# The last row group finished in two halves, and the fourth unit of x loaded ahead of the first matrix block

## The chip, the cores and the metric

The kernel runs on 1 core of one Trainium2 chip. The metric is the device time of one execution in microseconds (us). The kernel before takes 378.2 us (median of 3 runs, 377.26 to 378.64).

## The reference, cut to what matters

```python
# N = 5120 rows (2048 users, 3072 items), 64 features, adj is 5120 x 5120, all fp32
h = jnp.maximum(_layernorm(x, axis=-1), 0.0)              # first norm and relu
u = par_u[0] * par_u[1] * (diag_u[:, None] * h_u @ W_u) + h_u
i = par_i[0] * par_i[1] * (diag_i[:, None] * h_i @ W_i) + h_i
e = jnp.concatenate([u, i], axis=0)
o = adj @ (adj.T @ e)                                      # two products with the matrix
mu, var = jnp.mean(o, -1, keepdims=True), jnp.var(o, -1, keepdims=True)
layer = (o - mu) * jax.lax.rsqrt(var + 1e-5) * ln_gamma + ln_beta + h
result = x + layer
```

## The kernel before, in words

**Tiling.** The matrix is handled as 20 panels of 256 columns (`PANELS`, g = 0 to 19) and 5 groups of 1024 rows (`GROUPS`, m = 0 to 4). A block of one panel and one group is 1 MB, and one DMA brings it into `natural` (`load_natural(g, m)`). For each panel, TensorE makes t = panel.T @ e in 40 matmuls of 256 columns (`first`, L641, bank `t_acc`); VectorE centres t (`keep_t`) and ScalarE spreads it. Then the panel is used again for adj @ t. For row groups 0 to 3 (`TURNED`) VectorE turns the block in 32x32 pieces into `strips` (`turn_strips`, L458), and TensorE multiplies from there (`second_strips`, L670, four banks of `h_acc`). For row group 4 (`LOADED`) the turned block is loaded from memory a second time into `cols` (`load_cols`), and TensorE multiplies with it (`second_loaded`, L654, 4 matmuls of 512 columns into bank 4 of `h_acc`). Panels 0 to 3 and the last two are written out; the others run in a loop, two at a time.

**The start.** SyncE issues the loads in one queue, in the order of the code: x unit 0, the small inputs, block (0, 0), x units 3 and 4, block (1, 0), x unit 5, and the eight other blocks of panels 0 and 1, then the first `cols`. ScalarE issues x units 1 and 2. VectorE norms x in six units (`UNITS`, u = 0 to 5): row sums (L410), centring (L416), squares summed (L421), reciprocal (L429), and two steps that make e (L442, L448). Its order is written out by hand: the row sums and the centring of unit 3 stand ahead of the two steps that make e of unit 0. TensorE's first matmul on the matrix waits for e of unit 0.

**The end.** The last panel (19) meets row groups 0 to 3 in another way: its columns come turned from memory (`adj_last`), and `last_columns(m)` (L707) makes the last part of the sum of group m in a bank of its own. VectorE adds it to the rest (`out_sum`, L567), TensorE turns the sum so that rows lie on partitions (`out_turn`, L721), ScalarE squares (L392), VectorE sums the squares (L421), ScalarE takes the root (L314), VectorE takes the reciprocal (L429) and scales (`out_scale`, L583). Gamma is multiplied in by GpSimd for groups 0 and 2 (L293) and by VectorE for groups 1 and 3 (L576, ahead of the scaling). GpSimd adds x, h and beta, which lie ready in `xs` (L296), and SyncE stores the group. `scaled` has two buffers, so from group 2 on VectorE waits for GpSimd's addition of the group two before.

Group 4 comes last: after the last `second_loaded`, ScalarE squares it (L402), matmuls with `ones` sum the squares over the features (`last_var`, L730), VectorE multiplies by gamma where features lie on partitions (L594, `gamma_d`), TensorE turns the product (L721), and VectorE takes the reciprocal, scales (L583), adds (L598), and SyncE stores 256 KB. The lines that wait for the work before it are these:

```python
                if m >= 2:
                    dve.wait_ge(s_o_added, m - 1)      # also m = 4: the third addition on GpSimd
```

## Time and profile before

| what | value |
|---|---|
| median of 3 runs | 378.2 us (377.26 to 378.64) |
| profiled execution, its own time | 377.57 us |
| its span | 375.8 us |
| TensorE busy | 366.2 us (97%) |
| VectorE busy | 252.2 us (67%) |
| ScalarE busy | 73.4 us (20%) |
| GpSimd busy | 22.6 us (6%) |
| moved by DMA | 133.13 MB, mean 354 GB/s |

The span runs from the first to the last event that the profile shows. The execution's own time is 1.8 us more. PE is TensorE, PEld its weight load, DVE is VectorE, ACT is ScalarE, POOL is GpSimd, and SPq is the DMA queue of SyncE. A row of the timeline reads: start, duration, engine, line, operation, output and inputs, shapes, and how often. A bracket at its end is idle time of the engine just ahead of it, with what ended it. An fp32 matmul instruction leaves two records, a transpose one. Each timeline used here is that of one engine; records of one kind that follow each other are merged into one row.

### The profile page before, as it was taken

The numbers are of one execution on the slowest core, as the hardware profiler recorded it, in microseconds if no ns is written. First come the engines' busy times: TensorE is split into PE (matmuls) and PEld (weight loads), VectorE is DVE, ScalarE is ACT, GpSimd is POOL, SyncE is SP. The second block draws the span as 40 slices with busy tenths as digits, with TensorE's granted clock in tenths as the row PEclk, the third lists the DMA queues.
The fourth block names the chain that finished last, engine by engine and source line by source line (L and its number), as shares of the span: only waits on it lengthen the run. The fifth ranks groups of instructions, "written<-read, shape, count | busy, mean of one in ns | idle before, by whom it ended". The sixth has DMA issues, their size and how long they took to land.

```text
span 375.8 us, 9724 instructions
## 1 busy us (share of the span) xinstructions
PE 366.2 (97%) x4328; PEld 192.0 (51%) x4328; DVE 252.2 (67%) x242; ACT 73.4 (20%) x212; POOL 22.6 (6%) x29
## 2 busy tenths in 40 slices
PE   7899999999999999999999999999999999999994
PEld 4565454545643664465456436634654464456332
DVE  4999995759528933992496279339933982622476
ACT  5763022200220022003102200220022023002321
POOL 2024060000000000000000000000000000000035
PEclk9999999999999999999999999999999999999999
DMA  8999999999999999699959986996999599949003
GB/s 310 420 421 415 419 423 419 419 421 419 420 418 419 374 425 425 232 399 426 425 194 413 424 368 261 425 423 240 385 426 424 207 421 427 380 133 413 17 13 128
DMA packets 19746, 133.13 MB, mean 354 GB/s; under 512 B 2192, under 2 KB 2704, under 8 KB 3856
## 3 DMA queue, kind: packets, MB, share of 16 engines
q1 hardware_dynamic: 19440, 132.48, 86.2%
q10 hardware_dynamic: 288, 0.39, 0.3%
q8 instruction: 13, 0.21, 0.2%
q14 instruction: 5, 0.04, 0.0%
HBM read 131.55 MB, written 1.31 MB: 354 GB/s over the span
## 4 chain that ended last, share of the span: by engine, by line
PE 87%; DVE 6%; issue 1%; ACT 0%; DVEq 0%
PE t_acc L641 41%; PE h_acc L670 35%; PE h_acc L654 9%; DVE strips L458 2%; PE t_acc L707 1%; DVE var L421 1%; DVE scaled L583 1%; DVE e L442 1%; DVE natural L567 0%; PE h_acc L721 0%; DVE e L448 0%; DVE scaled L576 0%; DVE centred L471 0%; DVE rstd L429 0%; DVE xs L598 0%
## 5 line engine op out<-in xcount | busy, mean ns | idle before, releaser
L458 DVE STREAM_TRANSPOSE strips<-natural 128x2048 f32<-128x2048 f32 x76 | 168.2, 2275 | 49.3 <-PE h_acc L670 49.3
L641 PE MATMUL t_acc<-natural,e 128*64 128x256 f32 x1600 | 175.7, 380 | 0.7 <-DVE e L448 0.3
L641 PEld LDWEIGHTS t_acc<-natural,e 128*64 128x64 f32 x1600 | 114.3, 137 | 63.3 <-issue 6.3
L670 PE MATMUL h_acc<-strips,centred 32*64 32x512 f32 x2432 | 133.3, 589 | 0.1
L670 PEld LDWEIGHTS h_acc<-strips,centred 32*64 32x64 f32 x2432 | 53.4, 132 | 78.4 <-issue 77.9
L338 ACT COPY t_high<-t_acc 64x256 f32<-64x256 f32 x20 | 7.4, 368 | 211.7 <-PE t_acc L641 211.7
L466 DVE TENSOR_TENSOR t_sum<-t_acc,t_high 64x256 f32<-64x256 f32 x20 | 8.2, 410 | 56.3 <-ACT t_high L338 56.0
L654 PE MATMUL h_acc<-cols,centred 128*64 128x512 f32 x160 | 38.3, 599 | 0.0
L345 ACT COPY centred<-centred 32x384 f32<-32x384 f32 (+2 forms) x60 | 24.2, 403 | 67.3 <-DVE centred L479 66.8
L346 ACT COPY centred<-centred 32x128 f32<-32x128 f32 (+2 forms) x60 | 23.9, 398 | 0.0
L293 POOL TENSOR_TENSOR scaled<-scaled,smalls 128x512 f32<-128x512 f32 x2 | 2.5, 1270 | 310.6 <-DVE scaled L583 310.6
L654 PEld LDWEIGHTS h_acc<-cols,centred 128*64 128x64 f32 x160 | 10.5, 136 | 20.3 <-issue 19.1
L471 DVE STREAM_TRANSPOSE centred<-t_sum 32x256 f32<-32x256 f32 x40 | 17.3, 432 | 1.0
L479 DVE SCALAR_TENSOR_TENSOR centred<-t_total,centred 32x512 f32<-32x512 f32 x20 | 13.6, 679 | 0.7
L477 DVE TENSOR_REDUCE t_total<-centred 32x8 f32<-32x512 f32 x20 | 13.5, 674 | 0.7
L330 ACT ACTIVATE strips<-centred,rstd 128x64 f32<-128x64 f32 x40 | 10.0, 335 | 1.1 <-DVE rstd L429 1.1
L276 POOL TENSOR_TENSOR xs<-xs,strips 128x512 f32<-128x512 f32 x5 | 6.2, 1270 | 20.7 <-DVE e L448 20.7
L282 POOL TENSOR_TENSOR xs<-xs,smalls 128x512 f32<-128x512 f32 x5 | 6.2, 1282 | 14.5 <-issue 14.5
L421 DVE TENSOR_REDUCE var<-squares 128x8 f32<-128x512 f32 (+1 forms) x10 | 6.3, 627 | 0.8 <-ACT squares L392 0.5
L410 DVE TENSOR_REDUCE total<-xs 128x8 f32<-128x512 f32 (+1 forms) x6 | 3.6, 593 | 4.7 <-DMA xs<-x 4.6
L618 PE MATMUL h_acc<-ident,centred 128*128 128x128 f32 x20 | 3.8, 306 | 2.0 <-DVE centred L416 2.0
L629 PE MATMUL h_acc<-smalls,across 128*128 128x128 f32 x40 | 5.4, 283 | 0.3 <-ACT across L323 0.3
(53 smaller groups left out, 77.2 us busy)
## 6 DMA issues: line engine op xcount, KB each, us to landing
natural<-adj_rows SPq DMA_DIRECT2D x100, 1024.0 KB, 11.7
cols<-adj_cols SPq DMA_DIRECT2D x20, 1024.0 KB, 13.4
natural<-adj_last SPq DMA_DIRECT2D x4, 1024.0 KB, 7.2
out<-xs SPq DMA_DIRECT2D x5, 256.0 KB, 2.0
xs<-x SPq DMA_DIRECT2D x3, 256.0 KB, 7.4
xs<-x ACTq DMA_DIRECT2D x1, 256.0 KB, 3.5
smalls<-small SPq DMA_DIRECT2D x1, 150.0 KB, 3.2
xs<-x ACTq DMA_DIRECT2D x1, 128.0 KB, 2.9
```

Source lines behind the costliest of these rows:

```text
L330: last = nc.scalar.activation(h_in[:, k], centred_of(u)[:, n], ACT.Relu, scale=rstd[:, u % 2, n:n + 1])
L345: nc.scalar.copy(part[:, :, 0:QUADRANTS - q], t[0:Q, a, :, q:QUADRANTS])
L346: last = nc.scalar.copy(part[:, :, QUADRANTS - q:QUADRANTS], t[0:Q, a, :, 0:q])
L421: nc.vector.tensor_reduce(var[:, n % 2, 0:tiles], squares[:, n % 2, 0:tiles], AX.X, ALU.add).then_inc(s_var, 1)
L458: nc.vector.transpose(strips[:, a, :, m].rearrange("p c t i -> p t c i"), natural[:, a, m].rearrange("p t (c j) -> p t c j", j=Q)).then_in ...
L466: nc.vector.tensor_tensor(t_sum[:], t_acc[0:D, a, 0:WIDE], t_high[:], ALU.add).then_inc(s_t_sum, 1)
L471: last = nc.vector.transpose(t[0:Q, a, :, :, Q * d:Q * (d + 1)], t_sum[Q * d:Q * (d + 1), :].rearrange("p (b u j) -> p b u j", b=BLOCKS, j=Q))
L477: nc.vector.tensor_reduce(t_total[:], rows, AX.X, ALU.add).then_inc(s_t_total, 1)
L479: nc.vector.scalar_tensor_tensor(rows, t_total[:].unsqueeze(2).to_broadcast([Q, STRIPS, D]), -1.0 / D, rows, ALU.mult, ALU.add).then_inc(s ...
L641: last = nc.tensor.matmul(t_acc[D * s:D * (s + 1), a, 0:WIDE], e[:, GT * m + 2 * k + s, :], natural[:, a, m, HALF * s + k], start=(m == 0 ...
L654: last = nc.tensor.matmul(h_acc[D * s:D * (s + 1), LOADED], t[:, a, b, 0, :], cols[:, a, s, b], start=(isinstance(g, int) and g == 0 and b ...
L670: last = nc.tensor.matmul(h_acc[D * s:D * (s + 1), q], t[part, a, b, u, :], rows, start=(isinstance(g, int) and g == 0 and b == 0 and u == 0),
```

## The change

It has two parts. At the start, the load of x unit 3 is issued ahead of matrix block (0, 0). At the end:

- The 512 loaded columns of row group 4 are two parts of 256. Part 0 of the last two panels goes to a new bank, `late`; what had gathered for it before is copied out early (`kept`), and VectorE adds the two (`part_sum`). Part 1 stays in bank 4.
- Each part is squared, multiplied by gamma (on ScalarE, for both parts), turned, and finished by itself. The finish is a reciprocal and four `scalar_tensor_tensor` instructions of 64 elements (times reciprocal, plus `xs`), in the place of one scaling and one addition of 512. Each part is stored by itself (128 KB).
- The turning of group m on TensorE stands between the halves of `last_columns(m + 1)`, no longer behind the whole of it.
- Gamma of group 1 moves from VectorE to GpSimd.

```diff
             load_x(0)
             sp.dma_start(smalls[:, 0:GAMMA], small[:, 0:GAMMA]).then_inc(s_small, 16)
+            load_x(3)
             load_natural(0, 0)
-            load_x(3)
             load_x(4)
...
-            for m in range(GROUPS):
-                if m < LOADED:
-                    sp.wait_ge(s_o_added, m + 1)
-                else:
-                    sp.wait_ge(s_o_done, 1)
+            for m in range(TURNED):
+                sp.wait_ge(s_o_added, m + 1)
                 sp.dma_start(out[:, rows_of(m), :], xs[:, rows_of(m), :]).then_inc(s_out, 16)
+            for part in range(2):
+                sp.wait_ge(s_o_done, part + 1)
+                sp.dma_start(out[:, last_rows(part), :], xs[:, last_rows(part), :]).then_inc(s_out, 16)
...
-                if m % 2 == 0:
-                    nc.gpsimd.tensor_tensor(scaled[:, 0], scaled[:, 0], gamma_s.unsqueeze(1).to_broadcast([P, GT, D]),
+                if m < LOADED - 1:
+                    nc.gpsimd.tensor_tensor(scaled[:, m % 2], scaled[:, m % 2],
+                                            gamma_s.unsqueeze(1).to_broadcast([P, GT, D]),
                                             ALU.mult).then_inc(s_o_pool_gamma, 1)
...
+            def last_square(part, h):
+                nc.scalar.activation(across[:, 1, columns_of(part)], h, ACT.Square).then_inc(s_last_square, 1)
+
+            def last_gamma(part, h):
+                nc.scalar.activation(across[:, 0, columns_of(part)], h, ACT.Copy,
+                                     scale=gamma_d).then_inc(s_last_copy, 1)
...
             for m in range(TURNED):
                 square_out(m)
+                if m == TURNED - 1:
+                    act.wait_ge(s_part_sum, 1)
+                    last_square(0, h_part)
+                    act.wait_ge(s_norm, 16)
+                    last_gamma(0, h_part)
+                std(LATER + m)
+            act.wait_ge(s_part_done, 2)
+            last_square(1, h_acc[:, LOADED, columns_of(1)])
+            last_gamma(1, h_acc[:, LOADED, columns_of(1)])
+            for part in range(2):
+                act.wait_ge(s_last_var, part + 1)
+                nc.scalar.activation(var[:, 0, halves(part)], last_vars(part), ACT.Sqrt, bias=eps[:],
+                                     scale=1.0 / D).then_inc(s_std, 1)
...
+            def part_sum():
+
+                dve.wait_ge(s_part_done, 1)
+                dve.wait_ge(s_kept, 1)
+                nc.vector.tensor_tensor(h_part, late[:, columns_of(0)], kept, ALU.add).then_inc(s_part_sum, 1)
+
+            def last_rows_out(part):
+                n = LATER + LOADED + part
+                dve.wait_ge(s_std, n + 1)
+                nc.vector.reciprocal(rstd[:, 0, halves(part)], var[:, 0, halves(part)]).then_inc(s_rstd, 1)
+                dve.wait_ge(s_rstd, n + 1)
+                dve.wait_ge(s_o_turned, LOADED + part + 1)
+                for k in range(HALF):
+                    at = HALF * part + k
+                    row = xs[:, GT * LOADED + at]
+                    last = nc.vector.scalar_tensor_tensor(row, last_bank(part)[:, D * k:D * (k + 1)], rstd[:, 0, at:at + 1],
+                                                          row, ALU.mult, ALU.add)
+                last.then_inc(s_o_done, 1)
...
             out_scale(2)
+            part_sum()
             out_scale(3)
-            dve.wait_ge(s_last_square, 1)
-            nc.vector.tensor_scalar(across[:, 0], h_acc[:, LOADED], gamma_d, None, ALU.mult).then_inc(s_last_copy, 1)
-            out_scale(LOADED)
-            dve.wait_ge(s_o_scaled, GROUPS)
+            dve.wait_ge(s_o_added, LOADED - 1)
             dve.wait_ge(s_res, GROUPS)
-            nc.vector.tensor_tensor(xs[:, rows_of(LOADED), :], scaled[:, LOADED % 2], xs[:, rows_of(LOADED), :],
-                                    ALU.add).then_inc(s_o_done, 1)
+            for part in range(2):
+                last_rows_out(part)
...
-            last_columns(0)
-            last_columns(1)
-            out_turn(0)
-            last_columns(2)
-            out_turn(1)
-            last_columns(3)
-            out_turn(2)
-            second_loaded(LAST - 1, 0, LAST // 2)
-            out_turn(3)
-            second_loaded(LAST, 1, LAST // 2)
-            last_var()
-            out_turn(LOADED)
+            last_columns(0, range(BLOCKS))
+            for m in range(1, TURNED):
+                last_columns(m, range(1))
+                out_turn(m - 1)
+                last_columns(m, range(1, BLOCKS))
+            loaded_part(0, 0)
+            out_turn(TURNED - 1)
+            loaded_part(0, 1)
+            loaded_part(1, 0)
+            loaded_part(1, 1, range(1))
+            last_turn(0)
+            loaded_part(1, 1, range(1, BLOCKS))
+            for part in range(2):
+                last_var(part)
+            last_turn(1)
```

On TensorE, at the start of the end stage, the kernel before runs the columns of groups 0 and 1 (L707) whole, then the transposes of group 0 (L721):

```order
L707 MATMUL t_acc<-natural,centred 64x512 [waits s_t,s_t_sum,s_natural00]
L707 MATMUL t_acc<-natural,centred 64x512 x3
L707 MATMUL t_acc<-natural,centred 64x512 [waits s_natural01]
L707 MATMUL t_acc<-natural,centred 64x512 x3
L721 MATMUL h_acc<-ident,natural 128x128 [waits s_o_sum]
L721 MATMUL h_acc<-ident,natural 128x128 x3
```

In the changed kernel the same place of TensorE reads as follows (L776 is `last_columns`, L795 `out_turn`):

```order
L776 MATMUL t_acc<-natural,centred 64x512 [waits s_t,s_t_sum,s_natural00]
L776 MATMUL t_acc<-natural,centred 64x512 x3
L776 MATMUL t_acc<-natural,centred 64x512 [waits s_natural01]
L776 MATMUL t_acc<-natural,centred 64x512
L795 MATMUL h_acc<-ident,natural 128x128 [waits s_o_sum]
L795 MATMUL h_acc<-ident,natural 128x128 x3
L776 MATMUL t_acc<-natural,centred 64x512 x2
```

Four transposes that wait for the sum of group 0 now stand ahead of the last two matmuls of group 1. The same pattern comes again for groups 1 and 2.

On VectorE, the kernel before ends like this, from the squares of group 3 on:

```order
L421 TENSOR_REDUCE var<-squares 128x8 [waits s_squares]
L576 TENSOR_TENSOR scaled<-t_acc,smalls 128x512 [waits s_o_added]
L429 RECIPROCAL rstd<-var 128x8 [waits s_std]
L583 TENSOR_TENSOR scaled<-scaled,rstd 128x512 [waits s_o_gamma,s_rstd]
L594 TENSOR_SCALAR across<-h_acc,smalls 128x512 [waits s_last_square]
L429 RECIPROCAL rstd<-var 128x8 [waits s_std,s_o_added]
L583 TENSOR_TENSOR scaled<-h_acc,rstd 128x512 [waits s_o_turned,s_rstd]
L598 TENSOR_TENSOR xs<-scaled,xs 128x512 [waits s_res,s_o_scaled]
```

The changed kernel, from `part_sum` (L627) on, ends like this on the same engine (L460, L468, L616 and L621 are L421, L429, L576 and L583 of before):

```order
L627 TENSOR_TENSOR natural<-late,natural 128x256 [waits s_kept,s_part_done]
L460 TENSOR_REDUCE var<-squares 128x8 [waits s_squares]
L616 TENSOR_TENSOR scaled<-t_acc,smalls 128x512 [waits s_o_added]
L468 RECIPROCAL rstd<-var 128x8 [waits s_std]
L621 TENSOR_TENSOR scaled<-scaled,rstd 128x512 [waits s_o_gamma,s_rstd]
L632 RECIPROCAL rstd<-var 128x4 [waits s_std,s_res,s_o_added]
L638 SCALAR_TENSOR_TENSOR xs<-h_acc,rstd,xs 128x64 [waits s_o_turned,s_rstd]
L638 SCALAR_TENSOR_TENSOR xs<-h_acc,rstd,xs 128x64 x3
L632 RECIPROCAL rstd<-var 128x4 [waits s_std]
L638 SCALAR_TENSOR_TENSOR xs<-h_acc,rstd,xs 128x64 [waits s_o_turned,s_rstd]
L638 SCALAR_TENSOR_TENSOR xs<-h_acc,rstd,xs 128x64 x3
```

The gamma of group 4 (L594) is gone from VectorE. The wait for GpSimd's third addition (`s_o_added`) still stands ahead of the first reciprocal of group 4. Three instructions behind that wait have become ten.

## Rows read from the trace of the kernel before

**Rows 1.** The page: the span, and what the DMA engines moved in 40 equal slices.

```profile
span 375.8 us, 9724 instructions
GB/s 310 420 421 415 419 423 419 419 421 419 420 418 419 374 425 425 232 399 426 425 194 413 424 368 261 425 423 240 385 426 424 207 421 427 380 133 413 17 13 128
```

**Rows 2.** Timeline of PE, the first 36 us.

```profile
11.87 1.08 PE L641 MATMUL t_acc<-natural,e 128*64 128x256 f32 x8 [0.35 <-DVE e L448]
...
33.10 1.95 PE L641 MATMUL t_acc<-natural,e 128*64 128x256 f32 x16 [0.32 <-DMA natural<-adj_rows]
35.16 7.13 PE L670 MATMUL h_acc<-strips,centred 32*64 32x512 f32 x128
```

**Rows 3.** Timeline of DVE, the first 12 us, and 18 to 34 us.

```profile
9.40 0.69 DVE L410 TENSOR_REDUCE total<-xs 128x8 f32<-128x512 f32 x1 [1.14 <-DMA xs<-x]
...
18.82 0.16 DVE L436 TENSOR_TENSOR rstd_diag<-rstd,smalls 128x8 f32<-128x8 f32 x1
18.89 0.20 DVE L429 RECIPROCAL rstd<-var 128x8 f32<-128x8 f32 x1
...
32.76 11.06 DVE L458 STREAM_TRANSPOSE strips<-natural 128x2048 f32<-128x2048 f32 x5
```

**Rows 4.** Timeline of PE, the end stage.

```profile
359.07 0.66 PE L721 MATMUL h_acc<-ident,natural 128*128 128x128 f32 x4
359.66 1.94 PE L707 MATMUL h_acc<-natural,centred 128*64 128x512 f32 x8
```

**Rows 5.** Timeline of DVE, the end stage.

```profile
357.53 0.69 DVE L567 TENSOR_TENSOR natural<-t_acc,natural 128x512 f32<-128x512 f32 x1 [0.57 <-PE t_acc L707]
359.19 0.69 DVE L567 TENSOR_TENSOR natural<-t_acc,natural 128x512 f32<-128x512 f32 x1 [0.97 <-PE t_acc L707]
360.39 0.69 DVE L421 TENSOR_REDUCE var<-squares 128x8 f32<-128x512 f32 x1 [0.52 <-ACT squares L392]
...
364.31 1.39 DVE L583 TENSOR_TENSOR scaled<-scaled,rstd 128x512 f32<-128x512 f32 x1
...
370.20 0.74 DVE L594 TENSOR_SCALAR across<-h_acc,smalls 128x512 f32<-128x512 f32 x1
371.44 0.20 DVE L429 RECIPROCAL rstd<-var 128x8 f32<-128x8 f32 x1 [0.50 <-POOL xs L296]
371.76 0.69 DVE L583 TENSOR_TENSOR scaled<-h_acc,rstd 128x512 f32<-128x512 f32 x1
372.49 0.70 DVE L598 TENSOR_TENSOR xs<-scaled,xs 128x512 f32<-128x512 f32 x1
```

**Rows 6.** Timeline of POOL, the end stage.

```profile
362.52 1.27 POOL L293 TENSOR_TENSOR scaled<-scaled,smalls 128x512 f32<-128x512 f32 x1 [309.33 <-DVE scaled L583]
363.88 1.27 POOL L296 TENSOR_TENSOR xs<-scaled,xs 128x512 f32<-128x512 f32 x1
...
368.33 1.27 POOL L293 TENSOR_TENSOR scaled<-scaled,smalls 128x512 f32<-128x512 f32 x1 [1.28 <-DVE scaled L583]
369.68 2.95 POOL L296 TENSOR_TENSOR xs<-scaled,xs 128x512 f32<-128x512 f32 x2
```

**Rows 7.** Windows near the end; the last two columns are DMA share and GB/s.

```profile
373.00:373.50 0.50, 0.00 (x0) 0.00 (x0) 0.19 (x1) 0.00 (x0) 0.00 (x0) 1.00 0.05 16
373.50:374.00 0.50, 0.00 (x0) 0.00 (x0) 0.00 (x0) 0.00 (x0) 0.00 (x0) 1.00 0.99 369
...
374.50:375.00 0.50, 0.00 (x0) 0.00 (x0) 0.00 (x0) 0.00 (x0) 0.00 (x0) 0.50 0.76 283
```

**Rows 8.** Timeline of SyncE's queue, the last 12 us.

```profile
365.18 8.37 SPq L257 DMA_DIRECT2D out<-xs  x5
```

**Rows 9.** Groups by shape, whole span: busy, mean ns of one.

```profile
L330 ACT ACTIVATE strips<-centred,rstd 128x64 f32<-128x64 f32 x40 | 10.0, 335 | 1.1 <-DVE rstd L429 1.1
...
L448 DVE TENSOR_TENSOR e<-e,strips 128x512 f32<-128x512 f32 x4 | 2.8, 689 | 0.1
...
L448 DVE TENSOR_TENSOR e<-e,strips 128x256 f32<-128x256 f32 x2 | 0.8, 424 | 0.1
```

125 lines of the change are left out of this document (82 added, 43 removed).

## The prediction

> **What bounds the kernel now.** I read the page first: TensorE is 97% busy, and the DMA engines move some 420 GB/s over the first 120 us [rows 1]. I then looked only at the two places that the change touches, the first 35 us and the last 20. Everything between them stays as it is, and TensorE runs there without a gap that the waits show.
>
> At the start, VectorE idles 1.14 us at 9.40 for x unit 3, and behind that stands e of unit 0, for which TensorE starts its first matmuls on the matrix at 11.87 [rows 2, 3]. So unit 3 does hold back the first matmul. But a second wait comes later: at 33.10 TensorE idles 0.32 us for a matrix block, the last of panel 1, and only two row groups' worth (1.95 us) later does `second_strips` begin, at 35.16 [rows 2]. That block is the last of ten of 1.05 MB. With x (1.31 MB) and the small inputs (0.15 MB) 11.95 MB stand ahead of its landing. The four first slices of 9.4 us carry 310, 420, 421 and 415 GB/s [rows 1], so 12.8 MB have moved by 33.1 us. The queue has been full all the time: the block comes when the bytes ahead of it have come.
>
> At the end, the last step that waits is at 371.44: the reciprocal of group 4 idled 0.50 us for GpSimd's third addition [rows 5]. On GpSimd, gamma of group 0 starts at 362.52, gamma of group 2 at 368.33, and two additions fill 369.68 to 372.63 [rows 6]; the first of these ends at 371.41 and releases VectorE. Then come 0.20 us of reciprocal, a scaling at 371.76 and an addition that ends at 373.19. The last of the stores is issued at 373.22 (the queue's row ends at 373.55, less 0.33 of one issue; five issues share the row) [rows 8]. The stores of groups 3 and 4, 512 KB, move their bytes from 373.5 to 374.88: the window before has a share of 0.05, the window from 373.50 has 0.99, the one from 374.50 has 0.76 [rows 7]. The span ends at 375.8, 0.92 us after the last byte.
>
> **The start, step by step.** With unit 3 ahead of block (0, 0), its 0.26 MB no longer wait behind 1.05 MB. VectorE has its 1.14 us back, unless unit 3 still comes late (0.93 MB at 0.42 MB per us are 2.2 us of queue; it is needed at 8.3). So e of unit 0 and the first matmul come about 1.1 us earlier. All that TensorE does up to 33.10 can shift by as much. The last block of panel 1 can't: the same bytes stand ahead of it. TensorE then idles 0.32 + 1.1 = 1.4 us there, and the gain is gone. What is left: in the kernel before, VectorE's strips of block (0, 3), the first of five in the row at 32.76, end at about 35.05, together with TensorE [rows 3]. If VectorE is 1.1 us ahead, `second_strips` follows the matmuls directly, at some 35.0 instead of 35.16. I take −0.2 us. The bounds are 0 (the strips are late anyway) and −1.1 (the block lands earlier too, so that all of the shift is kept).
>
> **The end on TensorE.** The number of columns is the same. Halving the matmuls costs nothing by the rows: 16 records of 256 columns take 1.95 us [rows 2], 8 of 512 take 1.94 [rows 4]. What moves is `out_turn`. The transposes of group 0 take 0.59 us of TensorE (359.07 to 359.66) [rows 4]. They now stand ahead of the last two matmuls of group 1, and wait for VectorE's sum of group 0, ready at 358.22 [rows 5], while TensorE would be there at 358.1: a wait of 0.1 to 0.2. So group 1's columns are done not at 359.14 but 0.8 later, at 359.95. VectorE runs in order: the sum of group 1 (359.19 before, 360.0 now) stands ahead of group 0's sum of squares. The squares come earlier (the transposes do), but the sum of squares can start only 0.6 after the sum of group 1 does, at 360.6 instead of 360.39 [rows 5]. Group 0 is scaled 0.2 us later, though its transposes were moved up.
>
> **The end on GpSimd.** It has one instruction more, gamma of group 1. Up to the third addition it runs six of 1.27 us with gaps of up to 0.09 [rows 6]: 362.73 + 6 × 1.27 + 0.4 = 370.75. The kernel before had idle time in this stretch (1.28 us ahead of 368.33), which the new instruction fills. Then there is the port that the two engines share: VectorE's scaling of group 1, with both tensors in SBUF, took 1.39 us instead of 0.69 at 364.31, while GpSimd's addition ran to 365.15 [rows 5, 6], and GpSimd's addition at 369.68 took 1.73 because such a scaling ran. By my walk through the order, the scaling of group 3 is ready at 369.3, waits until gamma of group 2 ends at 369.4, and runs then; the third addition is held by 0.55 and ends at 371.3. Before, it ended at 371.41: −0.1. The fourth addition ends at 372.6 (372.63 before), so the store of group 3 is issued as before.
>
> **The end on VectorE.** Gamma of groups 1 and 4 goes (0.68 and 0.74 us), `part_sum` comes (0.42, by the 128x256 row [rows 9]). All that lies under the wait for GpSimd and moves nothing; `kept` lies in VectorE's idle time ahead of 355.66. ScalarE's two gammas and the last roots are ready by 371.2 in my walk, 0.1 us early: a thin cover, which costs its own excess if it fails. Behind the wait stand a reciprocal and four instructions, twice. The trace has no `scalar_tensor_tensor` of 128x64 with a pointer as scalar. By length: 0.689 at 512 and 0.424 at 256 [rows 9] give 0.0010 us per element, so 0.22 at 64. The pointer: L594, which has one, took 0.744 [rows 5], 0.06 more than its neighbours. I take 0.28 each. With no wait between, the next starts before the last ends: at 18.82 one of 0.16 is followed after 0.07 [rows 3]. So four take 3 × 0.19 + 0.28 = 0.85. The bounds are 3 × 0.13 + 0.22 = 0.61 (no pointer cost) and 4 × 0.335 = 1.34 (ScalarE's 128x64 with a pointer [rows 9], no overlap).
>
> The chain is then: 371.35 reciprocal; 371.67 first of the four (0.32 behind, as 371.44 to 371.76); end 372.52; the second reciprocal at 372.45; its four from 372.77 to 373.62. Before, VectorE ended at 373.19. That is 0.43 later (bounds 0.0 and 1.4).
>
> The Trainium skill (VectorE: DVE Perf Modes, The DRAIN you can't avoid) says that the next Vector instruction does not start until the pipe has emptied, and its rules for kernel authors say to minimize the number of instructions. By that rule, four would take 4 × 0.28 = 1.12 us, and the end would come 0.5 us later than in my sum; the row at 18.82 speaks against it here.
>
> **The stores.** Part 1's store is issued at 373.65. Store of group 3 and part 0 (384 KB) have the DMA engines from 373.5 to 374.54, at the 1.38 us that 512 KB took [rows 7]. Group 3's bytes moved 0.85 us after its issue (372.65 to 373.5), so part 1 can move from 374.5, just when they come free, to 374.88. This is the end of before. A VectorE up to 0.4 us late costs nothing, and one that is earlier gains nothing, since the fourth addition on GpSimd still sets when the last 512 KB begin. End: 0.0, bounds −0.1 and +1.0 (VectorE at its upper bound, 1.4 − 0.4).
>
> **Sum.** −0.2 (start) and 0.0 (end): 377.57 becomes 377.4 for the profiled execution. The median of the runs shown is 0.63 above that execution: 378.0.
>
> **The rivals.**
> 1. *The start's gain is kept.* For it: unit 3 is the wait at 9.40. It needs the last block of panel 1 to land 1.1 us earlier, with the same bytes ahead of it. 0.9 MB beyond these had moved by then, so landing isn't strictly in order, and a little may shift. 376.9, and 376.0 if the end gave 0.9 too. Chance 0.20.
> 2. *The small instructions cost more,* at the upper bound without overlap, or the last roots are late: +0.7 to +1.0, 379.0. Chance 0.12.
> 3. *Slower: the port.* The eight small instructions read and write `xs` in SBUF while the fourth addition runs (371.3 to 372.6). If they count as such a pair, they start at 372.6, 0.95 later, and with the upper price of each the end moves to 372.6 + 1.34 + 0.5 + 1.34 = 375.8, 2.2 us past the point from which it counts: 380.2. At my price of each it is 374.8, so 379.1. It decides from a start behind 372.0. For it: the 1.39 at 364.31. Against it: L594, with a pointer in SBUF, ran in its usual time at 370.20 beside GpSimd. The Trainium skill (SBUF — State Buffer, Terms) has the pair of ports locked for the whole of an instruction, the other engine blocked, which the 1.39 bears out. Chance 0.09.
> 4. *The interleaved transposes add up:* each of three waits 0.2 for VectorE, and scaling of all groups comes 0.6 later: 378.6. Chance 0.07.
>
> The forecast itself has 0.52. Its own range is 377.2 to 378.9, with the spread of the runs. Faster by over 0.5% would be below 376.3, slower above 380.1; 0.5% is about what a measurement of this kernel can tell from no change. Faster takes a third of rival 1 and a little from the rest: 0.09. Slower takes half of rival 3 and little more: 0.06. The range of 8 in 10 takes in most of rivals 1 and 2: 376.7 to 379.3.
>
> **What the profile of the changed kernel would show.** First matmul on the matrix at 10.8 with no idle of VectorE ahead of unit 3's row sums; then an idle of some 1.4 us for a block near 33.1, and `second_strips` at 35.0. If that row stands at 34.0, rival 1 is right. At the end: the first scaling 0.2 later, GpSimd without idle from 362.7 to its last addition but for the held one, the reciprocal of part 0 released by GpSimd at 371.1 to 371.3 (after the start's shift), small instructions of 0.22 to 0.34. A reciprocal released by ScalarE, or small instructions of over 0.5, would show the forecast wrong.

## The result and the profile after

The changed kernel takes 378.67 us (median of 17 executions, 377.9 to 379.25); the kernel before, taken beside it, 377.59 us (17 executions). The ratio is 1.002 with an interval of 1.0011 to 1.0029. The change costs 1.1 us (0.3%) by the medians and 0.8 us (0.4 to 1.1) by the ratio. The forecast was no change with a gain of 0.2 us within it. The profiled execution took 378.85 us, its span 377.0 us; what lies outside the span is 1.85 us in this one.

The page of the changed kernel, the two lines that answer to [rows 1]:

```profile
span 377.0 us, 9769 instructions
GB/s 263 427 417 417 420 423 418 421 421 417 421 420 418 365 428 424 244 395 429 421 213 411 429 356 249 428 423 242 359 428 422 227 388 427 407 146 408 11 14 127
```

The first slice of 9.4 us carries 263 GB/s where it was 310. The next twelve slices differ from those of before by at most 7 GB/s, in both directions. So the DMA engines fall behind by 0.44 MB in the first 9.4 us, and don't make it up in the slices behind it.

The changed kernel, timeline of TensorE, the first 36 us (columns as in [rows 2]; L696 is `first`, L727 `second_strips`):

```profile
10.57 1.08 PE L696 MATMUL t_acc<-natural,e 128*64 128x256 f32 x8 [0.26 <-DVE e L487]
...
29.30 1.95 PE L696 MATMUL t_acc<-natural,e 128*64 128x256 f32 x16 [0.40 <-DMA natural<-adj_rows]
31.79 1.95 PE L696 MATMUL t_acc<-natural,e 128*64 128x256 f32 x16 [0.54 <-DMA natural<-adj_rows]
34.35 1.95 PE L696 MATMUL t_acc<-natural,e 128*64 128x256 f32 x16 [0.61 <-DMA natural<-adj_rows]
36.22 7.12 PE L727 MATMUL h_acc<-strips,centred 32*64 32x512 f32 x128
```

The first matmul on the matrix comes at 10.57, 1.30 us earlier than in [rows 2]. Then TensorE waits for three blocks one after the other, where it waited once, and `second_strips` begins at 36.22, not at 35.16: 1.06 us later. The next view says what happened to the blocks.

The changed kernel, windows at the start (columns: PE busy, PEld, DVE, ACT, POOL, granted clock, DMA share, GB/s):

```profile
2.00:10.00 8.00, 6.74 (x43) 4.37 (x40) 6.21 (x15) 5.47 (x17) 0.70 (x2) 1.00 0.97 338
5.00:6.00 1.00, 0.91 (x6) 0.43 (x4) 1.00 (x3) 0.49 (x2) 0.07 (x1) 1.00 1.01 217
10.00:28.00 18.00, 16.90 (x141) 11.08 (x141) 16.40 (x31) 12.31 (x45) 2.27 (x2) 1.00 1.02 422
```

From 2 to 10 us the DMA engines moved 338 GB/s; the kernel before moved 394 there, and 401 between 5 and 6 us, where the changed one has 217. The share of busy time is about 1 in both (0.97 and 1.00 from 2 to 10 us). By the share the engines were taken, but they brought fewer bytes. From 10 us on the rate is 422, as before (421).

On VectorE the row sums of unit 3 no longer wait (they start at 8.12), but those of unit 5 do:

```profile
13.10 0.69 DVE L449 TENSOR_REDUCE total<-xs 128x8 f32<-128x512 f32 x1 [1.26 <-DMA xs<-x]
```

So VectorE's lead is gone again: its strips that began at 32.76 in [rows 3] begin at 32.63.

The changed kernel, timeline of TensorE at the end stage (L776 is `last_columns`, L795 `out_turn`):

```profile
356.54 2.80 PE L776 MATMUL t_acc<-natural,centred 128*64 128x512 f32 x12
359.33 0.65 PE L795 MATMUL h_acc<-ident,natural 128*128 128x128 f32 x4
359.92 1.08 PE L776 MATMUL t_acc<-natural,centred 128*64 128x512 f32 x4
```

The end stage starts at 356.54, where the kernel before had 355.49: the 1.05 us of the start, carried through the whole kernel without a change. For the end I therefore compare times counted from this row. The end stage lasts 20.46 us up to the end of the span, and 20.31 before.

The changed kernel, timeline of VectorE, the last 5 us ([rows 5] of before):

```profile
369.50 0.68 DVE L616 TENSOR_TENSOR scaled<-t_acc,smalls 128x512 f32<-128x512 f32 x1
370.10 0.19 DVE L468 RECIPROCAL rstd<-var 128x8 f32<-128x8 f32 x1
370.32 1.78 DVE L621 TENSOR_TENSOR scaled<-scaled,rstd 128x512 f32<-128x512 f32 x1
372.03 0.16 DVE L632 RECIPROCAL rstd<-var 128x4 f32<-128x4 f32 x1
372.23 0.86 DVE L638 SCALAR_TENSOR_TENSOR xs<-h_acc,rstd,xs 128x64 f32<-128x64 f32 x4
373.01 0.17 DVE L632 RECIPROCAL rstd<-var 128x4 f32<-128x4 f32 x1
373.21 0.86 DVE L638 SCALAR_TENSOR_TENSOR xs<-h_acc,rstd,xs 128x64 f32<-128x64 f32 x4
```

The changed kernel, timeline of GpSimd, the same stretch ([rows 6] of before):

```profile
368.93 1.28 POOL L316 TENSOR_TENSOR scaled<-scaled,smalls 128x512 f32<-128x512 f32 x1
370.29 1.26 POOL L320 TENSOR_TENSOR xs<-scaled,xs 128x512 f32<-128x512 f32 x1
372.19 1.26 POOL L320 TENSOR_TENSOR xs<-scaled,xs 128x512 f32<-128x512 f32 x1 [0.63 <-DVE scaled L621]
```

GpSimd's third addition starts at 370.29, VectorE's scaling of group 3 at 370.32. Both have their tensors in SBUF. The addition runs in its usual 1.26, the scaling takes 1.78 where one alone takes 0.69. The last stretch of VectorE is then released by its own scaling, no longer by GpSimd: the reciprocal at 372.03 has no idle ahead of it. VectorE ends at 374.07, or 17.53 after the start of the stage; before it was 373.19, or 17.70.

The changed kernel, timeline of SyncE's queue, the last stores (L277 stores groups 0 to 3, L280 the two parts):

```profile
366.42 7.39 SPq L277 DMA_DIRECT2D out<-xs  x4
373.85 1.40 SPq L280 DMA_DIRECT2D out<-xs  x2
```

The changed kernel, windows at the end (columns as above):

```profile
374.50:375.00 0.50, 0.00 (x0) 0.00 (x0) 0.00 (x0) 0.00 (x0) 0.00 (x0) 0.50 0.94 356
375.00:375.50 0.50, 0.00 (x0) 0.00 (x0) 0.00 (x0) 0.00 (x0) 0.00 (x0) 0.50 0.51 172
375.50:376.00 0.50, 0.00 (x0) 0.00 (x0) 0.00 (x0) 0.00 (x0) 0.00 (x0) 0.50 0.79 262
376.00:377.00 1.00, 0.00 (x0) 0.00 (x0) 0.00 (x0) 0.00 (x0) 0.00 (x0) 0.50 0.17 55
```

The issues by line say how long each of them took (minimum, median and maximum in ns, then the start of the first and of the last):

```profile
L280 SPq DMA_DIRECT2D out<-xs x2: 439/676/912, 373.8 to 374.8; - x2
L277 SPq DMA_DIRECT2D out<-xs x4: 332/338/348, 366.4 to 373.5; - x4
```

A store of 256 KB takes 0.34 us to issue. Those of the two halves take 0.91 and 0.44. The row of 1.40 runs from 373.85 to 375.25, and the last of the two starts at 374.8, so the long one is part 0's. The share falls to 0.51 between the stores of part 0 and part 1. So VectorE was 0.17 earlier, counted from the stage's start, and the span 0.15 later.

A third piece doesn't show in any row. The time of an execution less its span is 1.75 to 2.00 us in all 134 executions of the kernel before whose span is known, with a mean of 1.86 to 1.92 by batch. (One of them took 994.47 us and is in none of the medians and ratios.) In the changed kernel it is over 2.2 in 6 of 17 (up to 2.9), with a mean of 2.17. The median of the spans is 376.2 for the changed kernel and 375.6 to 375.7, by batch, for the kernel before (its 17 executions above have no spans on record). So the median execution has 0.6 more of span and about 0.3 more outside it. Together that is 0.9, between the 0.8 of the ratio and the 1.1 of the medians. The profiled execution has 1.2 more of span, 1.05 from the start and 0.15 from the end: the start cost more in it than in the middle one.

### The profile page after: what moved, and what is told of

Same layout as the page of the kernel before. It is cut to its first block, busy times and chain, and to the rows that moved or that the text cites. A ratio compares the mean times of both kernels' runs of the same rounds, so it can differ in the third digit from the quotient of the medians.

```text
span 377.0 us, 9769 instructions
## 1 busy us (share of the span) xinstructions
PE 366.9 (97%) x4344; PEld 192.3 (51%) x4344; DVE 252.2 (67%) x249; ACT 74.3 (20%) x216; POOL 23.4 (6%) x30
## 4 chain that ended last, share of the span: by engine, by line
PE 87%; DMA 7%; DVE 2%; SPq 2%; issue 1%; ACT 0%; DVEq 0%
PE t_acc L696 42%; PE h_acc L727 35%; PE h_acc L710 9%; DMA natural<-adj_rows 7%; SPq L230 1%; PE t_acc L776 1%; PE h_acc L776 1%; DVE var L460 0%; DVE scaled L621 0%; SPq L227 0%; DVE xs L638 0%; DVE natural L608 0%; PE h_acc L795 0%; ACT var L338 0%; DVE scaled L616 0%
## 5 line engine op out<-in xcount | busy, mean ns | idle before, releaser
L696 PE MATMUL t_acc<-natural,e 128*64 128x256 f32 x1600 | 176.2, 380 | 1.8 <-DMA natural<-adj_rows 1.6
L696 PEld LDWEIGHTS t_acc<-natural,e 128*64 128x64 f32 x1600 | 114.1, 137 | 65.1 <-issue 6.3
L727 PE MATMUL h_acc<-strips,centred 32*64 32x512 f32 x2432 | 133.3, 589 | 0.0
L727 PEld LDWEIGHTS h_acc<-strips,centred 32*64 32x64 f32 x2432 | 52.9, 132 | 78.7 <-issue 77.9
L710 PE MATMUL h_acc<-cols,centred 128*64 128x512 f32 x144 | 34.4, 598 | 0.0
L316 POOL TENSOR_TENSOR scaled<-scaled,smalls 128x512 f32<-128x512 f32 x3 | 3.8, 1275 | 310.7 <-DVE scaled L621 310.7
L710 PEld LDWEIGHTS h_acc<-cols,centred 128*64 128x64 f32 x144 | 9.5, 136 | 18.9 <-issue 17.6
L460 DVE TENSOR_REDUCE var<-squares 128x8 f32<-128x512 f32 (+1 forms) x10 | 6.3, 626 | 0.3 <-ACT squares L334 0.2
L684 PEld LDWEIGHTS h_acc<-smalls,across 128*128 128x128 f32 x40 | 4.8, 191 | 2.0 <-ACT across L347 1.3
```

Source lines behind the costliest of these rows:

```text
L684: last = nc.tensor.matmul(unit_bank(u)[:, P * b:P * (b + 1)], across[:, u % 2, P * b:P * (b + 1)], wdiag[:, int(lo >= N_USERS // P)], star ...
L696: last = nc.tensor.matmul(t_acc[D * s:D * (s + 1), a, 0:WIDE], e[:, GT * m + 2 * k + s, :], natural[:, a, m, HALF * s + k], start=(m == 0 ...
L710: last = nc.tensor.matmul(h_acc[D * s:D * (s + 1), LOADED], t[:, a, b, 0, :], cols[:, a, s, b], start=(isinstance(g, int) and g == 0 and b ...
L727: last = nc.tensor.matmul(h_acc[D * s:D * (s + 1), q], t[part, a, b, u, :], rows, start=(isinstance(g, int) and g == 0 and b == 0 and u == 0),
```

## The experiments

Each median stands beside that of the kernel before, taken on the same chip, with the ratio's interval. "Span" is the median of the spans of all executions, 9 to 12 of each kernel. "Outside" is the mean of an execution's time less its span. Three chips were used: one for e1 to e4, one for e5 to e8 and e13 to e16, one for e9 to e12.

### Which half of the change costs: e1 and e2

`e1_after_x3_back` is the changed kernel with x unit 3 behind the block again:

```diff
-            load_x(3)
             load_natural(0, 0)
+            load_x(3)
             load_x(4)
```

> The changed kernel with x unit 3 back behind matrix block (0, 0); the end stage stays changed. Theory 'start' (with unit 3 ahead, the DMA engines move some 0.4 MB less in the first 9 us though they are busy, so the last block of panel 1 lands 1.2 us later and TensorE waits for it): TensorE's last matmuls of panel 1 (34.35 us in the changed kernel) are back at about 33.1, the first slice of the page is back at some 310 GB/s, and the time is 0.9 to 1.2 us under the changed kernel, 0 to 0.3 over the kernel before. Theory 'end' (the timed difference comes from the end stage, and the late block is chance of one execution): the time stays at 1.0 over the kernel before. Theory 'both': half and half, 0.5 over.

`e2_before_x3_ahead` is the kernel before with that one line moved forward:

```diff
+            load_x(3)
             load_natural(0, 0)
-            load_x(3)
             load_x(4)
```

> The kernel before with x unit 3 ahead of matrix block (0, 0) and nothing else. Theory 'start': 0.9 to 1.2 us slower than the kernel before, with TensorE waiting for matrix blocks 0.4 to 0.6 us three times between 29 and 35 us. Theory 'end': no change within 0.2 us.

Measured: e1 377.91 against 377.57, ratio 1.0011 (1.0000 to 1.0023), span 375.8. e2 378.11 against 377.57, ratio 1.002 (1.001 to 1.0029), span 376.2. By the spans the line alone costs what the whole change costs (376.2 in both); by the medians it costs 0.54 us, half of it. I had expected 0.9 to 1.2 us and three waits for blocks; there are two. Windows of e2 (columns as above):

```profile
2.00:10.00 8.00, 6.32 (x42) 4.16 (x39) 6.08 (x15) 5.46 (x16) 0.69 (x2) 1.00 0.93 345
5.00:6.00 1.00, 0.50 (x4) 0.20 (x2) 1.00 (x3) 0.73 (x3) 0.20 (x1) 1.00 0.71 246
```

The loss of bytes is there too, and in e1 it is not: 376 GB/s from 2 to 10 us and 434 from 5 to 6. Timeline of TensorE in e2, the last block of panel 1:

```profile
33.71 1.95 PE L641 MATMUL t_acc<-natural,e 128*64 128x256 f32 x16 [0.61 <-DMA natural<-adj_rows]
35.59 7.12 PE L670 MATMUL h_acc<-strips,centred 32*64 32x512 f32 x128
```

`second_strips` begins 0.43 later than before here, and at 35.10 in e1. The end stage of e1 lasts 20.08 us in its profile, 0.23 less than before; by the median of its spans, 375.8 against 375.6, nothing of that remains. What e1 still loses, 0.3 us, lies outside the span: 2.26 in the mean, five of eleven executions over 2.2; e2 has 1.90 and none. A difference of this size in the medians says little by itself: `e6_names_only`, further down, does the same work as the kernel before and has 0.34 us more.

### Why the blocks come later: e4, e5, e9 and e10

Theory: x unit 3 directly ahead of block (0, 0) makes the queue carry fewer bytes. Rival: any x unit that is moved forward delays the blocks by its own bytes. Four orders of the kernel before tell these apart. In e4 all three units stand ahead:

```diff
+            load_x(3)
+            load_x(4)
+            load_x(5)
             load_natural(0, 0)
-            load_x(3)
-            load_x(4)
             load_natural(1, 0)
-            load_x(5)
```

> The kernel before with x units 3, 4 and 5 all ahead of the first matrix block. Theory 'pieces': loads of x (pieces of 2 KB and less) that follow each other without a matrix block (pieces of 8 KB) between them move fewer bytes per time. Then this order loses more than unit 3 alone: the last block of panel 1 lands 2 us or more later, time +1.5 to +3. Rival 'one collision' (the loss belongs to the place where unit 3 and unit 2 of the other queue meet): the loss stays at about 1.0. Rival 'bytes' (only the bytes ahead count): no change.

In e5 unit 3 is taken out of SyncE's queue and issued by ScalarE:

```diff
             load_natural(0, 0)
-            load_x(3)
...
-            for u in (1, 2):
+            for u in (1, 2, 3):
                 act.dma_start
```

> The kernel before with x unit 3 issued by ScalarE, behind its units 1 and 2, so that matrix block (0, 0) stays first in SyncE's queue. Theory 'alternation' (the loss comes from SyncE's order unit 3, block, unit 4, block, unit 5: moved all ahead, the units cost nothing): no loss here, the first slice stays at 300 to 310 GB/s, span as before (375.6 median) or down to 0.2 less, since VectorE gets unit 3 early. Theory 'unit 3 early' (whatever brings unit 3 in before block (0, 0) costs): the span rises by 0.6 as with unit 3 ahead.

In e9 units 3 and 4 stand ahead:

```diff
+            load_x(3)
+            load_x(4)
             load_natural(0, 0)
-            load_x(3)
-            load_x(4)
             load_natural(1, 0)
```

> The kernel before with x units 3 and 4 ahead of block (0, 0) in SyncE's queue, unit 5 still behind block (1, 0). With unit 3 alone ahead the DMA engines move 340 to 345 GB/s from 2 to 10 us and the span rises by 0.6; with units 3, 4 and 5 ahead 380, and nothing is lost. If the loss comes from a block that follows one unit of x and is followed by another (unit, block, unit, block, unit), this order has it once and not twice: 355 to 375 GB/s, span +0.2 to +0.4. If it comes from unit 5 between the blocks, the loss is whole: +0.6. If it belongs to unit 3 directly ahead of block (0, 0), none: 375 to 390 GB/s and a span within 0.2.

In e10 only unit 3 does, and unit 4 goes behind block (1, 0):

```diff
+            load_x(3)
             load_natural(0, 0)
-            load_x(3)
-            load_x(4)
             load_natural(1, 0)
+            load_x(4)
             load_x(5)
```

> The kernel before with x unit 3 ahead of block (0, 0), and units 4 and 5 behind block (1, 0). If the loss belongs to unit 3 directly ahead of block (0, 0), it is whole here: 335 to 355 GB/s from 2 to 10 us, span +0.5 to +0.7. If it comes from unit 4 between the two blocks, it is gone: 375 to 390 GB/s. Units 4 and 5 come later for VectorE, which may wait 1 to 2 us for unit 4; the wait for the last block of panel 1 hides that, unless e of the later groups comes late for TensorE.

The table holds the result of each and its windows; "start" is the start of `second_strips` in the profile. e3, which stands under "The stores", has the start of the changed kernel. The ten others are e1, e6 to e8 and e11 to e16, whose edits leave the order of the loads as it was before.

| order | median, before | ratio (interval) | span | GB/s 2 to 10 us | GB/s 5 to 6 us | start |
|---|---|---|---|---|---|---|
| before | | | 375.6 | 394 | 401 | 35.16 |
| after | 378.67, 377.59 | 1.002 (1.0011 to 1.0029) | 376.2 | 338 | 217 | 36.22 |
| the ten others with the order of before | | | | 373 to 397 | 369 to 451 | 34.81 to 35.61 |
| e3, unit 3, changed end | 378.13, 377.57 | 1.0019 (1.0005 to 1.0034) | 376.2 | 346 | 279 | 36.55 |
| e2, unit 3 | 378.11, 377.57 | 1.002 (1.001 to 1.0029) | 376.2 | 345 | 246 | 35.59 |
| e10, unit 3, then two blocks | 379.43, 377.63 | 1.0042 (1.0023 to 1.006) | 377.55 | 355 | 270 | 35.69 |
| e9, units 3 and 4 | 377.78, 377.63 | 0.9999 (0.9985 to 1.0014) | 375.8 | 381 | 412 | 34.90 |
| e4, units 3, 4, 5 | 377.63, 377.57 | 1.0002 (0.9993 to 1.0012) | 375.75 | 380 | 381 | 35.17 |
| e5, unit 3 by ScalarE | 377.66, 377.49 | 1.0003 (0.9994 to 1.0013) | 375.7 | 388 | 430 | 35.22 |

The two windows of e9, and under them those of e10:

```profile
2.00:10.00 8.00, 6.74 (x42) 4.21 (x39) 6.04 (x15) 5.31 (x16) 0.70 (x2) 1.00 1.00 381
5.00:6.00 1.00, 0.92 (x6) 0.44 (x4) 1.00 (x3) 0.33 (x2) 0.28 (x1) 1.00 1.17 412
```

```profile
2.00:10.00 8.00, 7.37 (x33) 4.68 (x30) 6.12 (x15) 4.53 (x13) 0.70 (x2) 1.00 0.96 355
5.00:6.00 1.00, 1.00 (x6) 0.52 (x4) 1.00 (x3) 0.33 (x2) 0.24 (x1) 1.00 0.84 270
```

The rival falls: e4 puts three units ahead, 0.79 MB, and loses nothing. The dip belongs to the orders in which exactly one unit stands between the small inputs and block (0, 0): four profiles with 217 to 279 GB/s between 5 and 6 us, against 369 and more in the fourteen others. With a second unit behind it, or with the first in another queue, it is not there. In e2, e3 and e10 part of the loss is idle time (shares of 0.71, 0.89 and 0.84 between 5 and 6 us), in the changed kernel it isn't (1.01). The share isn't a strict fraction of time: it reads 1.17 in a window of e9.

The column "start" needs more care, since it is one execution of each kernel. With the order of before it varies by 0.8 us (34.81 to 35.61), and 35.59 (e2) and 35.69 (e10) lie at the edge of that; 36.22 and 36.55 lie outside it. What the order costs in time is therefore better read from the spans of e2, +0.6. e10 loses most in its median, more than its start in the profile explains. There unit 4 comes late too, and VectorE waits for it. Timeline of VectorE in e10:

```profile
12.25 0.69 DVE L410 TENSOR_REDUCE total<-xs 128x8 f32<-128x512 f32 x1 [1.16 <-DMA xs<-x]
```

Its spans range from 376.3 to 378.5, and the profiled execution is the shortest of them, so the rest of that loss isn't seen in a row.

None of these orders gains. e9 has the first matmul early and nearly all of the bytes, and yet the last block of panel 1 comes when it did before. Timeline of TensorE in e9:

```profile
10.74 1.08 PE L641 MATMUL t_acc<-natural,e 128*64 128x256 f32 x8 [0.26 <-DVE e L448]
...
33.02 1.95 PE L641 MATMUL t_acc<-natural,e 128*64 128x256 f32 x16 [0.58 <-DMA natural<-adj_rows]
```

It is the same in e4 (first matmul at 10.65, `second_strips` at 35.17). In e5, unit 3 is early too (row sums at 8.44 without a wait), but the first matmul comes at 11.71, so there is little to lose. Timeline of TensorE in e5:

```profile
33.34 1.95 PE L640 MATMUL t_acc<-natural,e 128*64 128x256 f32 x16 [0.59 <-DMA natural<-adj_rows]
35.22 7.12 PE L669 MATMUL h_acc<-strips,centred 32*64 32x512 f32 x128
```

That is the part of the prediction that held: what is gained ahead of the first matmul is lost at this block. The kernels with the order of before say the same without any edit there. VectorE's wait for unit 3 was 1.14 us in the profile of [rows 3], but it is 0 in e7 and e14 and 1.49 in e16. Their first matmuls come at 10.71, 10.80 and 12.31, and `second_strips` at 35.02, 34.87 and 35.61: of the 1.5 to 1.6 us that lie between them at the first matmul, 0.6 to 0.7 are left. So the wait that the change was to remove isn't there in every execution.

### The parts of the end: e7, e8, e15, e14 and e13

`e7_order_and_gamma` is the kernel before with the transposes between the halves of `last_columns` and gamma of group 1 on GpSimd; group 4 is finished as before.

```diff
-                if m % 2 == 0:
-                    nc.gpsimd.tensor_tensor(scaled[:, 0], scaled[:, 0], gamma_s.unsqueeze(1).to_broadcast([P, GT, D]),
+                if m < LOADED - 1:
+                    nc.gpsimd.tensor_tensor(scaled[:, m % 2], scaled[:, m % 2], gamma_s.unsqueeze(1).to_broadcast([P, GT, D]),
...
-            last_columns(1)
-            out_turn(0)
-            last_columns(2)
-            out_turn(1)
-            last_columns(3)
-            out_turn(2)
+            for m in range(1, TURNED):
+                last_columns(m, range(1))
+                out_turn(m - 1)
+                last_columns(m, range(1, BLOCKS))
```

> The kernel before with two parts of the changed end: the transposes of group m between the halves of the columns of group m + 1, and gamma of group 1 on GpSimd; group 4 is finished whole, as before. By my walk the first scaling comes 0.2 later, GpSimd's third addition runs at once and the scaling of group 3 waits for it, so that VectorE's gamma of group 4 and its end come later: end stage 20.4 to 20.9 us from the first columns of group 0 to the end of the span, against 20.31; time 0.1 to 0.6 over before. If executions with over 2.2 us outside the span appear here, they belong to these two parts; if not, to the halves of group 4.

`e8_halves_only` is e1 without these two: group 4 in halves, two stores, the transposes behind the whole of `last_columns`, gamma of group 1 on VectorE.

```diff
-                if m < LOADED - 1:
+                if m % 2 == 0:
                     nc.gpsimd.tensor_tensor(
...
-                last_columns(m, range(1))
-                out_turn(m - 1)
-                last_columns(m, range(1, BLOCKS))
+                last_columns(m, range(BLOCKS))
+                out_turn(m - 1)
```

> The changed kernel with x unit 3 back, the transposes of a group behind the whole columns of the next, and gamma of group 1 on VectorE, as in the kernel before: what is left of the change is group 4 in two halves. The first scaling is back 0.2 earlier, the scaling of group 1 waits for GpSimd again (1.39 us). If it is the halves that gain at the end (0.2 us of span in the kernel with unit 3 back), the end stage is 20.0 to 20.2. Executions with over 2.2 us outside the span: 3 or more of 11 if they belong to the halves, none if to the other parts.

Measured: e7 378.47 against 377.49, ratio 1.0023 (1.0013 to 1.0033), span 376.5. e8 378.5, ratio 1.0028 (1.0018 to 1.0037), span 376.7. Each half of the end alone costs 0.9 to 1.1 us of span, and both together (e1) 0.2 or less. I had expected 0.1 to 0.6 us for e7 and an end stage of 20.0 to 20.2 us for e8, which has 21.57 in its profile: both were missed. Timeline of VectorE in e7:

```profile
369.14 1.76 DVE L583 TENSOR_TENSOR scaled<-scaled,rstd 128x512 f32<-128x512 f32 x1
370.83 0.74 DVE L594 TENSOR_SCALAR across<-h_acc,smalls 128x512 f32<-128x512 f32 x1
...
372.71 0.69 DVE L583 TENSOR_TENSOR scaled<-h_acc,rstd 128x512 f32<-128x512 f32 x1 [1.03 <-PE h_acc L723]
```

With one more instruction GpSimd starts its third addition at 369.10, 0.04 ahead of VectorE's scaling of group 3, and VectorE is held for 1.1 us. Gamma of group 4 stands behind that scaling on VectorE, the last transposes wait for it on TensorE, and VectorE waits for those: 1.03 us. In the changed kernel that gamma is on ScalarE, so the hold delays nothing but VectorE's own end. In e8 the scaling of group 3 starts 14.60 us after the stage's start (13.79 in e1, 14.10 before), since VectorE has both gamma of group 1 and `part_sum` ahead of it. GpSimd's addition is 0.23 us ahead of it (369.50), and it is held all the same. VectorE then ends 0.63 us later against the stage's start than before, and from there to the end of the span it is 3.24 us where it was 2.61; that second part is taken up under "The stores". Timeline of VectorE in e8:

```profile
369.73 1.58 DVE L621 TENSOR_TENSOR scaled<-scaled,rstd 128x512 f32<-128x512 f32 x1
...
372.60 0.86 DVE L638 SCALAR_TENSOR_TENSOR xs<-h_acc,rstd,xs 128x64 f32<-128x64 f32 x4
```

`e15_small_finish` is the kernel before, with eight instructions of 64 elements in the place of the last scaling and addition, and one store:

```diff
-            out_scale(LOADED)
...
-            nc.vector.tensor_tensor(xs[:, rows_of(LOADED), :], scaled[:, LOADED % 2], xs[:, rows_of(LOADED), :],
-                                    ALU.add).then_inc(s_o_done, 1)
...
+            for k in range(GT):
+                row = xs[:, GT * LOADED + k]
+                last = nc.vector.scalar_tensor_tensor(row, out_bank(LOADED)[:, D * k:D * (k + 1)], rstd[:, 0, k:k + 1],
+                                                      row, ALU.mult, ALU.add)
+            last.then_inc(s_o_done, 1)
```

> The kernel before with group 4 finished by one reciprocal and eight instructions of 128x64 in the place of a scaling and an addition, stored once. Eight take 7 x 0.19 + 0.28 = 1.6 us by the row of four in 0.86, against 1.43 before: VectorE ends 0.2 later, span +0.1 to +0.3. Theory 'VectorE' (it is these instructions, or their number): 3 or more of 11 executions with over 2.2 us outside; by the run with wide halves, which had 6 of 12, I expect none.

`e14_gamma_on_scalar` is the kernel before with gamma of group 4 on ScalarE:

```diff
+            nc.scalar.activation(across[:, 0], h_acc[:, LOADED], ACT.Copy, scale=gamma_d).then_inc(s_last_copy, 1)
...
-            nc.vector.tensor_scalar(across[:, 0], h_acc[:, LOADED], gamma_d, None, ALU.mult).then_inc(s_last_copy, 1)
```

> The kernel before with gamma of group 4 on ScalarE (an activation of 128x512 behind the square) in the place of VectorE's instruction. The transposes of group 4 can start at 370.4 instead of 371.0, but the reciprocal still waits for GpSimd's third addition at 371.4, so the span stays within 0.15 of before. Theory 'ScalarE' (one activation more with a pointer as scale): 3 or more of 11 executions with over 2.2 us outside. Rival: none.

`e13_columns_in_halves` is the kernel before with the loaded columns of the last two panels in matmuls of 256:

```diff
...
+                for part in range(2):
+                    at = slice(WIDE * part, WIDE * (part + 1))
+                    for b in range(BLOCKS):
+                        for s in range(2):
+                            last = nc.tensor.matmul(h_acc[D * s:D * (s + 1), LOADED, at], t[:, a, b, 0, :],
+                                                    cols[:, a, s, b, at], start=False,
...
```

> The kernel before, with the loaded columns of the last two panels multiplied as 256 and 256 (16 matmul instructions for 8) into the same bank, and nothing else. By the rows halving costs TensorE nothing: span within 0.1 of before. Theory 'TensorE' (the longer program of TensorE makes the close longer at times): 3 or more of 11 executions with over 2.2 us outside the span. Rival 'elsewhere': none.

Measured against 377.5: e15 377.48, ratio 1.0002 (0.9993 to 1.0011), span 375.7; e14 377.49, ratio 1.0002 (0.9993 to 1.0012), span 375.6. Neither moves the time. Timeline of VectorE in e15, and under it of e14, the same place:

```profile
371.25 0.20 DVE L429 RECIPROCAL rstd<-var 128x8 f32<-128x8 f32 x1 [0.50 <-POOL xs L296]
371.58 1.63 DVE L601 SCALAR_TENSOR_TENSOR xs<-h_acc,rstd,xs 128x64 f32<-128x64 f32 x8
```

```profile
371.15 0.20 DVE L431 RECIPROCAL rstd<-var 128x8 f32<-128x8 f32 x1 [1.16 <-POOL xs L296]
```

Eight small instructions take 1.63 us, and the two of 512 elements with the wait between took 1.43 (371.76 to 373.19, [rows 5]). In e14 the 0.74 us that VectorE no longer needs become idle time: 1.16 where [rows 5] have 0.50. e13 gives 377.76, ratio 1.0023 (1.0007 to 1.0039). The matmuls themselves cost nothing, as this row of TensorE shows:

```profile
364.70 1.95 PE L668 MATMUL h_acc<-cols,centred 128*64 128x256 f32 x16
```

The median is 0.27 higher, the mean more, since 5 of 12 spans are 376.8 to 378.4. I have no row that says why. For this step the run is inconclusive.

### The stores: e3, e11 and e12

`e3_one_store` is the changed kernel with one store of 256 KB behind both parts:

```diff
-            for part in range(2):
-                sp.wait_ge(s_o_done, part + 1)
-                sp.dma_start(out[:, last_rows(part), :], xs[:, last_rows(part), :]).then_inc(s_out, 16)
+            sp.wait_ge(s_o_done, 2)
+            sp.dma_start(out[:, rows_of(LOADED), :], xs[:, rows_of(LOADED), :]).then_inc(s_out, 16)
...
```

> The changed kernel with row group 4 stored once (256 KB, when both parts are done) in the place of two stores of 128 KB. In the changed kernel the issue of part 0's store took 0.91 us and that of part 1 0.44, where the 256 KB stores take 0.33, so that part 1's bytes move only from 375.25. Theory 'small stores cost': the store is issued at 374.1, takes 0.33, lands 2.0 to 2.4 later, and the time is 0.3 to 0.6 us under the changed kernel. Rival 'issue is held by the store before it, whatever the size': the one store's issue takes 0.7 or more and the time is within 0.2 us of the changed kernel.

`e12_x3_back_one_store` is e1 with the same edit, so that the start is that of before:

> The changed kernel with x unit 3 back and group 4 stored once. Theory 'small stores': the span is 0.1 to 0.3 under that with unit 3 back and two stores, so 375.5 to 375.7, level with the kernel before; the time is over before only by the executions with more outside the span, 0 to 0.4. Rival 'no price': the span stays at 375.8.

`e11_halves_wide` is e1 with each part finished by a scaling and an addition of 256 elements:

```diff
-                for k in range(HALF):
-                    at = HALF * part + k
-                    row = xs[:, GT * LOADED + at]
-                    last = nc.vector.scalar_tensor_tensor(row, last_bank(part)[:, D * k:D * (k + 1)], rstd[:, 0, at:at + 1],
-                                                          row, ALU.mult, ALU.add)
...
+                nc.vector.tensor_tensor(scaled[:, 0, halves(part)], last_bank(part).rearrange("p (k d) -> p k d", d=D),
+                                        by_tile(rstd[:, 0, halves(part)]), ALU.mult).then_inc(s_o_scaled, 1)
+                dve.wait_ge(s_o_scaled, LOADED + part + 1)
+                nc.vector.tensor_tensor(rows, scaled[:, 0, halves(part)], rows, ALU.add).then_inc(s_o_done, 1)
```

> The changed kernel with x unit 3 back, and each half of group 4 finished by one scaling and one addition of 128x256 (and a wait between them) in the place of four instructions of 128x64. By the rows, 0.42 + 0.04 + 0.42 = 0.88 against 0.86: time and span as with unit 3 back (span 375.8 median, within 0.3). Executions with over 2.2 us outside the span: if they belong to the eight small instructions, which have no waits between them, none here; if to the halves otherwise, 3 to 5 of 11.

Measured: e3 378.13 against 377.57, ratio 1.0019 (1.0005 to 1.0034), span 376.2, the median of the changed kernel (in the mean 0.17 below it, which is within the scatter). e12 377.55 against 377.63, ratio 0.9994 (0.998 to 1.0008), span 375.3: 0.5 below e1, and 0.4 below the kernel before. But `e16_more_at_the_close`, in the next part, has one store too, and its span is 376.2. So the runs don't show that one store is better than two.

The rows say where these kernels part. In the changed kernel, e1, e3, e12 and e16 VectorE ends 17.51 to 17.54 us after the start of the end stage, all alike. From there to the end of the span it is 2.93 and 2.56 us with two stores (the changed kernel, e1) and 2.52, 3.08 and 3.53 with one (e3, e12, e16). The short ones are those in which each issue of the last stores was short: 0.45 and 0.43 in e1, 0.33 in e3, against 0.91 (part 0), 0.94 and 0.79. The end of e8 (3.24, with 0.86 for part 0) fits that, the end of e11 (2.80, with 1.42 for part 0) less so. Why an issue takes long isn't known; there is one profile of each kernel, and e12's is its longest execution (span 376.2). e12 doesn't beat the kernel before all the same, since 6 of its 12 executions have over 2.2 us outside the span (mean 2.27). e11 gives 378.37, ratio 1.0006 (0.999 to 1.0021), span 375.8, as e1. What its rows show is the port that VectorE and GpSimd share. Timeline of VectorE in e11:

```profile
371.30 0.42 DVE L636 TENSOR_TENSOR scaled<-h_acc,rstd 128x256 f32<-128x256 f32 x1
371.76 1.04 DVE L639 TENSOR_TENSOR xs<-scaled,xs 128x256 f32<-128x256 f32 x1
...
373.38 0.42 DVE L639 TENSOR_TENSOR xs<-scaled,xs 128x256 f32<-128x256 f32 x1
```

The first addition, with both tensors in SBUF, stands beside GpSimd's last one and takes 1.04; the second, alone, 0.42. The small instructions of the changed kernel, which take one tensor from PSUM, ran beside the same addition (372.19 to 373.45) in 0.86 for four, and 0.86 again after it. The timeline of VectorE in e12, which has them too:

```profile
371.28 0.86 DVE L637 SCALAR_TENSOR_TENSOR xs<-h_acc,rstd,xs 128x64 f32<-128x64 f32 x4
...
372.26 0.86 DVE L637 SCALAR_TENSOR_TENSOR xs<-h_acc,rstd,xs 128x64 f32<-128x64 f32 x4
```

### The time outside the span: e6 and e16

Which part of the change carries the 0.3 us outside the span? Executions with over 2.2 us there: 29 of 74 in the kernels with the halved end (the changed kernel, e1, e3, e8, e11, e12), none of 98 in e2, e4, e5, e7, e9, e10, e14, e15 and e6, 1 of 12 in e13 (2.25), none of 134 before. So it is none of these by itself: the interleaving, the gamma on GpSimd or ScalarE, the small instructions, the second store. The span and the time outside it aren't independent either: in the changed kernel the six long ones have spans of 375.9 to 376.6, and the five executions with spans of 376.8 and more have 1.80 to 1.95 outside. `e6_names_only` declares the changed kernel's new semaphores and its bank in the kernel before, and uses none:

```diff
+        s_kept = sem("s_kept")
+        s_part_done = sem("s_part_done")
+        s_part_sum = sem("s_part_sum")
...
+        late = ps("late", [P, BANK])
```

> The kernel before with the three semaphores and the PSUM bank of the changed kernel declared and not used. The kernels with the changed end spend 2.3 to 3.0 us outside the span in 5 of 17, 5 of 11 and 4 of 11 executions, and 1.8 to 2.1 in the others; those with the end of before spend 1.75 to 2.0 in all 54. Theory 'declared' (more semaphores in use make the close of the program longer at times): executions with over 2.2 us outside the span here too, 3 or more of 11. Rival 'work' (it is something in the instructions of the changed end): none, and time and span are those of before.

`e16_more_at_the_close` is e12 with six tiny matmuls behind TensorE's last transposes; their results are not used:

```diff
             last_turn(1)
+            for k in range(6):
+                nc.tensor.matmul(late[:, WIDE + 2 * k:WIDE + 2 * k + 2], ident[:], ones[:], start=True, stop=True)
```

> The changed kernel with x unit 3 back and one store, and six matmuls of 2 columns into the free half of the new bank behind TensorE's last transposes. They run while VectorE finishes, and cost the span nothing: 375.3 as without them. Theory 'place' (the executions with more outside the span hang on where TensorE's program ends): their share moves clearly, to 0 or to nearly all of 11. Rival 'not TensorE': about 4 to 6 of 11, as before.

Measured: e6 377.83 against 377.49, ratio 1.0008 (0.9997 to 1.0018), 1.90 outside and none over 2.2: the names aren't it. e16 377.97 against 377.5, ratio 1.001 (1.0001 to 1.002); none of 11 executions is over 2.2 and the mean is 1.80, the least of all kernels. At the share of 29 in 74, eleven in a row without one have a chance of about 0.004 (45/74 to the power of 11). But the share isn't the same in all of these kernels. e8, the only one on e16's chip, has 2 of 11, and at that share the chance is 0.11. That six matmuls for which nobody waits took the long ones away is thus likely and not shown; e12 on the same chip would decide it. Nothing was gained by it: the span's median is 376.2, 0.9 above e12's, where I had expected 375.3. In e16's profile VectorE ends as in e12's (17.54 and 17.53 us after the stage's start), but its last three stores land 2.9 to 3.7 us after their issue, where e12's take 2.0 to 2.7. So the loss lies in the stores, as under "The stores". Neither its mechanism nor that of the long ones is settled.

## Why the prediction was wrong

**The start: the step that failed.** "The queue has been full all the time: the block comes when the bytes ahead of it have come." The term's worst case was 0, since I took the rate to be independent of the order. It is not: with unit 3 directly ahead of block (0, 0) the queue carried 338 GB/s and not 394 from 2 to 10 us. That is 0.45 MB over the 8 us, and at 422 GB/s it takes 1.07 us to make up, about the 1.06 us by which `second_strips` came late. The fit is closer than it should be: the same sum gives 0.93 us for e2 and 0.91 for e3, where the start came 0.43 and 1.39 us later. Forecast −0.2, measured +1.06 in the profile and +0.6 in the medians of spans (e2). The first slice of [rows 1], 310, is below its neighbours mostly because 12 GB/s move in the first 2 us, in both kernels; no row of the kernel before warned of the dip. That the order is the cause is shown by three pairs that differ in this line alone (before and e2, +0.6 of span; e1 and the changed kernel, +0.4; e12 and e3, +0.9, on two chips) and by e4, e5, e9 and e10. What happens in the queue or in the engines is not: the changed kernel brings fewer bytes at a full share, e2 also has a lower share (0.93). I have no experiment that looks below the queue.

**The start: what held.** The first matmul at 10.57 (forecast 10.8) and VectorE without idle ahead of the row sums at 8.12. The last block takes the gain back. Rival 1, a gain that is kept, would have had `second_strips` at 34.0; it is refuted by e4 and e9, which have the early first matmul and the bytes, and `second_strips` at 35.17 and 34.90. The term of −0.2 fits these two profiles (0 and −0.26), but their spans don't show a gain. One part of the walk failed even so: VectorE was to be 1.1 us ahead at the strips of 32.76, and was 0.13 ahead, since unit 5 came late (1.26 us at 13.10). And the 1.95 us ahead of `second_strips` are one row group's worth (16 records are 8 matmuls of the panel's 40), not two.

**The end on TensorE.** Counted from the stage's start, the scaling of group 0 came 0.2 later (6.39 us behind it, 6.20 before), as walked. Halved matmuls cost nothing (e13's row). Rival 4, waits that add up over the groups, is refuted: the scaling of group 3 came 13.78 us behind the stage's start, and 14.10 before.

**The end on GpSimd and VectorE.** My walk had the scaling of group 3 win the port, run in its 0.69 and hold the third addition by 0.55. It was ready when I said (370.32 less the 1.05 of the start is 369.27, forecast 369.3). But I had GpSimd's gamma of group 2 end at 369.4, and it ended at 369.16 on the same scale, since GpSimd's gaps were smaller than the 0.4 in my sum. So the addition began 0.03 us ahead of the scaling, and the hold fell on VectorE: 1.78. Then GpSimd's fourth addition waits for that scaling (0.63), which I had not at all. By luck little changes in the sum: the first reciprocal of group 4 comes at 372.03, released by VectorE, and VectorE ends 0.17 earlier than before against the stage, where I had 0.43 later. The step failed because two ready times 0.1 us apart decided it, in a walk whose error is larger; both outcomes should have been priced.

The Trainium skill (SBUF — State Buffer, Terms) says that the shared pair of ports is held for a whole instruction and that the loser is blocked fully. The 1.78 for an instruction of 0.69 beside an addition of 1.26, and e11's 1.04 for one of 0.42, agree with it.

**The small instructions.** Sized at 0.28 each and 0.85 for four; measured 0.276 to 0.284 and 0.86. Rival 2 is refuted at its price, rival 3 by the row at 372.23, which ran in 0.86 beside GpSimd's fourth addition.

The rule of the Trainium skill that the prediction cites (VectorE: DVE Perf Modes, The DRAIN you can't avoid) has an exception in the same paragraph, which the prediction left out: a next instruction that isn't held starts earlier. The row of 0.86 for four agrees with the exception and not with the 1.12 of the bare rule, and so does e15's of 1.63 for eight, where the bare rule would give 2.2.

**The stores.** I let VectorE be late within the 0.85 us between issue and bytes, and gave the issue its 0.33. The issue of part 0 took 0.91 and that of part 1 0.44; the bytes had a hole at 375.0 to 375.5. End term: forecast 0.0, measured +0.15 in the profile and +0.2 in the medians of e1's spans (0 in the means). The term was within its bounds, by luck: VectorE was 0.6 us earlier than forecast, and the stores took that back for a reason that wasn't in the term.

**Outside the span.** I took 1.8 us as a constant. It is not for this end: +0.3 in the mean. No term of the prediction held it.

**The sum.** +0.6 for the start, 0 to 0.2 for the end and 0.3 outside make 0.9 to 1.1 us, where 1.1 (medians) or 0.8 (ratio, 0.4 to 1.1) were measured. The median, 378.67, lies inside the range, but the range was set from the median of three runs of the kernel before, 378.2, and seventeen give 377.59: from there the forecast of −0.2 would be 377.4, and the measured time is 1.3 above it. The likeliest case, 378.0 by a gain of 0.2, did not come about, and the start's term is the one that had the wrong sign.

## What to carry to other kernels

Moving one load ahead of another keeps the bytes but may not keep the rate: after any change to a queue's order, compare the GB/s of the first slices, and try the order with two such loads ahead or the load in another queue. When two engines that share a port are ready within a few tenths of each other, price both outcomes, and look for what is queued behind the one that loses: gamma of group 4 behind a held scaling made e7 0.9 us slower, while the same hold cost nothing once that gamma was on ScalarE. Before a wait at the start is worth an edit, read it in several executions: this one was 0 to 1.49 us long in kernels with the same order of loads. And compare kernels on differences that are larger than what unused names make here, 0.34 us.

## What the runs showed of the hardware

- With one 0.26 MB load directly ahead of a 1.05 MB load in one queue, the DMA engines moved 338 to 355 GB/s from 2 to 10 us (after, e2, e3, e10); with two or three ahead, or with that load in another queue, or behind, 373 to 397 (14 kernels). I had expected the rate to depend on the bytes alone.
- The issue of a store of 128 KB took 0.43 to 1.42 us (0.91 and 0.44 in the changed kernel, 0.45 and 0.43 in e1, 0.86 and 0.44 in e8, 1.42 and 0.43 in e11, part 0 first), and that of the last one of 256 KB 0.33 in e3 but 0.94 in e12 and 0.79 in e16.
- Which of two engines gets the port was decided by an arrival 0.02 to 0.05 us earlier: GpSimd's addition was that much ahead in the changed kernel, e1, e3, e7, e11, e12 and e16, and VectorE took 1.76 to 1.79 us for an instruction of 0.69. In the kernel before VectorE was 0.09 us ahead, and GpSimd's addition took 1.73 instead of 1.27.
- An instruction on VectorE with one tensor in PSUM, one in SBUF and a pointer in SBUF wasn't held beside GpSimd's addition: four took 0.86 us beside it and 0.86 after it.
- The time between the span and the execution's own time was 1.75 to 2.0 us in 134 of 134 executions of one kernel and 2.33 to 3.04 in 29 of 74 of six kernels whose last row group is finished in halves.
